# Attention's order per engine rewritten around the DVE and POOL passes of a pair

## What is computed

```python
def attn(x):                                   # x = layer norm of the input, 16 x 256 x 128
    xn = layer_norm(x, gamma_in)
    q, k, v = xn @ Wq, xn @ Wk, xn @ Wv        # 16 heads of 64
    attn = softmax(causal(q @ k.T * scale))
    out  = attn @ v
    adj  = clip(attn + eye(n), 0, 1)
    deg  = adj.sum(-1)
    feats = v
    for l in range(2):
        h = adj @ (feats @ gnn_w[l] + gnn_b[l]) / deg
        feats = gelu(h + feats)
    out = out + feats @ lin_w + lin_b
    return layer_norm(out @ Wo, gamma_out)
x = x + attn(layernorm(x))
x = x + moe(layernorm(x))                      # 8 experts, hidden 352, top 2 of softmax(router)
```

## Time and profile before

| | us |
|---|---|
| median of 3 runs | 1221.41 |
| lowest and highest | 1219.86, 1223.13 |
| the profiled execution, its own time | 1227.73 |
| its span, first to last instruction | 1226.0 |

### The profile page before, as it was taken

The page is one execution under the profiler, slowest core; times in us unless marked ns, Lnnn a source line. Parts: engine busy times, 40 slices in busy tenths (PEclk is TensorE's granted clock), DMA queues, the critical chain, the costliest instruction groups (busy, mean ns, idle before and its releaser), DMA issues.

```text
span 1226.0 us, 28122 instructions
## 1 busy us (share of the span) xinstructions
PE 1102.3 (90%) x8320; PEld 862.3 (70%) x8320; DVE 967.5 (79%) x3755; ACT 797.4 (65%) x2351; POOL 509.9 (42%) x648
## 2 busy tenths in 40 slices
PE   6999989898989999999999999999999986798994
PEld 4777767676767676766766677667676764797993
DVE  6869797979797979797979797979798884466555
ACT  6776767676667676676757675767675752464652
POOL 4425252626252525252534343434343343444444
PEclk9999999999999999999999999999999987998997
DMA  6950000000000000000000000000000012121227
GB/s 205 406 196 1 2 10 2 9 1 9 1 9 1 7 3 5 5 2 8 0 10 0 10 0 9 1 9 1 9 1 9 2 33 66 47 62 54 66 60 217
DMA packets 37311, 47.41 MB, mean 39 GB/s; under 512 B 6009, under 2 KB 28539, under 8 KB 37200
## 3 DMA queue, kind: packets, MB, share of 16 engines
q1 hardware_dynamic: 32880, 37.81, 9.7%
q0 software_dynamic: 4320, 8.47, 2.1%
HBM read 18.14 MB, written 28.58 MB: 38 GB/s over the span
## 4 chain that ended last, share of the span: by engine, by line
PE 53%; DVE 34%; issue 7%; ACT 2%; another core or an unknown queue 2%; DMA 1%; POOL 1%; DVEq 0%; SPq 0%; ACTq 0%; POOLq 0%
PE bank L628 45%; DVE ea L1400 8%; DVE eb L1403 7%; DVE nmax L1388 7%; PE bank L997 2%; DVE dT L1417 2%; DVE t L1648 2%; PE bank L764 1%; PE bank L725 1%; DVE wgt L1412 1%; DVE next_row L1770 1%; PE bank L979 1%; DVE rs L1398 1%; DVE z L1437 1%
## 5 line engine op out<-in xcount | busy, mean ns | idle before, releaser
L495 POOL TENSOR_TENSOR ea<-ea,wgt 128x256 f32<-128x256 f32 x128 | 79.7, 622 | 439.5 <-DVE wgt L1412 439.5
L1388 DVE TENSOR_REDUCE nmax<-bank 128x1 f32<-128x128 f32 (+1 forms) x512 | 151.4, 348 | 61.7 <-PE bank L628 54.7
L1113 ACT ACTIVATE ea<-bank,nmax 128x128 f32<-128x128 f32 x256 | 98.0, 383 | 83.9 <-DVE nmax L1388 55.3
L1400 DVE SCALAR_TENSOR_TENSOR ea<-ident,ssum,ea 128x128 f32<-128x128 f32 x256 | 142.7, 593 | 0.0
L628 PE MATMUL bank<-gt,vnat 128*64 128x256 f32 (+1 forms) x1024 | 113.6, 343 | 31.7 <-ACT gvT L1081 31.7
L1403 DVE SCALAR_TENSOR_TENSOR eb<-idw,ssum,eb 128x256 f32<-128x256 f32 x256 | 141.7, 588 | 0.0
L497 POOL TENSOR_TENSOR eb<-eb,wgt 128x512 f32<-128x512 f32 x128 | 135.9, 1062 | 0.0
L628 PEld LDWEIGHTS bank<-gt,vnat 128*64 128x64 f32 x1024 | 68.3, 139 | 84.4 <-issue 41.7
L1113 ACT ACTIVATE eb<-bank,nmax 128x256 f32<-128x256 f32 x256 | 125.2, 489 | 0.0
L1081 ACT ACTIVATE gt<-bank 128x512 f32<-128x512 f32 (+1 forms) x256 | 111.7, 495 | 20.1 <-remote 19.8
L628 PE MATMUL bank<-gt,g 128*64 128x256 f32 (+1 forms) x1024 | 115.2, 347 | 4.9 <-DVE z L1443 3.8
(11 more groups left out here) (231 smaller groups left out, 3164.6 us busy)
## 6 DMA issues: line engine op xcount, KB each, us to landing
slots<-zero SPq DMA_DIRECT2D x33, 520.0 KB, 14.9
zin<-slots SPq DMA_DIRECT2D x71, 65.0 KB
got<-pairs SPq DMA_DIRECT2D x8, 512.0 KB, 7.0
raw_gu<-in_guT SPq DMA_DIRECT2D x8, 352.0 KB, 3.0
out<-x_all SPq DMA_DIRECT2D x8, 256.0 KB, 2.6
pairs<-zout,zin POOLq DMA_INDIRECT x71
dn<-in_downT SPq DMA_DIRECT2D x2, 512.0 KB, 16.1
slots<-z,row_now POOLq DMA_INDIRECT x64
```

The lines of the kernel that those rows point to most:

```text
L495: nc.gpsimd.tensor_tensor(ea[:, s], ea[:, s], wgt[:, s, 0:2].unsqueeze(2).to_broadcast([P, 2, P]), ALU.mult)
L1113: done = nc.scalar.activation(e[:, s, a, :], score_bank(n, a)[:, TILE_SCORES[t]], ACT.Exp, bias=nmax[:, s, i:i + 1], accum_out=ssum[:, s, ...
L1388: done = V.tensor_reduce(nmax[:, n % 3, i:i + 1], score_bank(n, a)[:, TILE_SCORES[t]], X, ALU.max, negate=True)
L1400: V.scalar_tensor_tensor(ea[:, s, a, :], ident[:, :], ssum[:, s, a:a + 1], ea[:, s, a, :], ALU.mult, ALU.max, accum_out=den[:, s, a:a + 1])
```

## The change

The lists of calls in `batch` are written in another order on POOL, PE, ACT and DVE. No call is added or dropped, but for these: `gelu2(n)` for n of 4 and more now waits on a new semaphore `s_og`, which PE's `output_graph` raises (it frees the slot of `f2T`), and `layer1(b, 0)` waits for the last copy of `qk` (both use bank 0). `output_attended(4)` moves from the next batch's list into the batch's own.

On DVE, `weights(n)` of pair 0 stands right behind `adjacency(0)`, the adjacencies of pairs 1 and 2 stand together, and other DVE work is put between a `weights(n)` and the next `adjacency`. The output of `before` is taken up earlier (`output_bias`, `output_kept`), and so are its norms and the next batch's input norm. The core of the diff for DVE and POOL, and what differs in ACT and PE by more than order:

```diff
@@ def batch of POOL
+                graph(b, 0)
+                degrees(b, 0)
+                graph(b, 1)
+                degrees(b, 1)
+                graph(b, 2)
+                graph(b, 3)
+                degrees(b, 2)
+                degrees(b, 3)
+                graph(b, 4)
+                if after is not None:
+                    deviation(after, 0, 3)
+                if before is not None:
+                    token_power(before, 0)
+                degrees(b, 4)
...
+                graph(b, 5)
...
+                        scatter(routed, c)
+                degrees(b, 5)
+                graph(b, 6)
+                graph(b, 7)
+                degrees(b, 6)
...
+                    for e in range(0, 3):
+                        gate_up_low(e)
                 if before is not None:
                     token_power(before, 1)
...
@@ PE
                 a_d.wait(pe, b, n + 1)
-                if n >= 1:
+                if n == 0:
+                    a_qk.wait(pe, b, PAIRS)
+                else:
                     d_z1.wait(pe, b, n)
...
-                product(bank[7][:, 0:TOKENS], lwo[:, n, :], f2T[:, n % 4, :], False, False)
+                product(bank[7][:, 0:TOKENS], lwo[:, n, :], f2T[:, n % 4, :], False, False).then_inc(s_og.sem, 1)
@@ ACT
                 d_z2.wait(act, b, n + 1)
+                if n >= 4:
+                    s_og.wait(act, b, n - 3)
@@ def batch of DVE
                 maxima(b, 1, 0)
+                adjacency(b, 0)
+                weights(b, 0)
                 maxima(b, 1, 1)
-                adjacency(b, 0)
-                maxima(b, 2, 0)
-                weights(b, 0)
...
                 if before is None:
                     small_weights()
                     dve.wait_ge(w_x, 16)
                 if after is not None:
                     norm_step(after, 0)
+                maxima(b, 2, 0)
+                maxima(b, 2, 1)
+                adjacency(b, 1)
+                adjacency(b, 2)
+                weights(b, 1)
+                if after is not None:
+                    norm_step(after, 1)
+                maxima(b, 3, 0)
+                weights(b, 2)
+                maxima(b, 3, 1)
+                if before is not None:
+                    output_bias(before)
+                if routed is not None:
+                    choose(routed, 2)
+                if before is not None:
+                    output_kept(before)
+                difference(b, 0)
+                attended(b, 0)
+                adjacency(b, 3)
```

More of the change, by code:

```diff
@@ L854, in batch @@
                 scores(b, 4)
-                differences(b, 0)
-                transposes(b, 1)
+                differences(b, 1)
+                if routed is not None:
+                    places(routed, bank[7][:, PLACES], before)
+                degrees(b, 1)
+                transposes(b, 2)
                 queries_keys(b, 6)
@@ L936, in batch @@
                 if after is not None:
-                    queries_keys(after, 1)
+                    values(after, 0, b)
             def tokens_transposed(p, o, free=None):
@@ L1236, in batch @@
                 if after is not None:
-                    queries_keys(after, 1)
+                    values(after, 0)
             def tokens_transposed(p, o):
@@ new lines, in batch @@
+                if before is not None:
+                    output_kept(before)
+                difference(b, 0)
+                attended(b, 0)
+                adjacency(b, 3)
+                maxima(b, 4, 0)
+                weights(b, 3)
+                maxima(b, 4, 1)
+                difference(b, 1)
+                if routed is not None:
+                    take_places(routed, bank[7][:, PLACES])
+                attended(b, 1)
+                if routed is not None:
+                    place_tokens(routed, 0)
+                    place_tokens(routed, 1)
@@ new lines, in batch @@
+                if before is not None:
+                    norm_tokens(before, 0)
+                maxima(b, 5, 0)
+                adjacency(b, 4)
+                difference(b, 2)
+                weights(b, 4)
+                if before is None:
+                    folded_values()
+                attended(b, 2)
+                maxima(b, 5, 1)
+                if before is not None:
+                    norm_tokens(before, 1)
+                maxima(b, 6, 0)
+                maxima(b, 6, 1)
@@ new lines, in batch @@
+                adjacency(b, 5)
+                difference(b, 3)
+                weights(b, 5)
+                attended(b, 3)
+                maxima(b, 7, 0)
+                maxima(b, 7, 1)
+                layer1_out(b, 0)
+                if after is not None:
+                    norm_step(after, 2)
+                adjacency(b, 6)
+                layer1_out(b, 1)
+                difference(b, 4)
+                attended(b, 4)
+                weights(b, 6)
+                layer1_out(b, 2)
@@ L1530, in batch @@
+                adjacency(b, 7)
+                if before is not None:
+                    norm_tokens(before, 2)
+                layer2_out(b, 0)
+                if after is None:
+                    gate_up_high(0)
+                if after is not None:
+                    norm_step(after, 3)
+                layer1_out(b, 3)
+                if after is None:
+                    table_first(0)
+                weights(b, 7)
                 difference(b, 5)
                 if after is not None:
-                    norm_step(after, 1)
```

301 lines of the change are left out of this document (107 added, 194 removed).

## The result

The changed kernel takes 1183.06 us (median of 4 runs, 1182.0 to 1185.7) where the kernel before takes 1221.86 beside it: a ratio of 0.9687, with a 95% interval from 0.9666 to 0.9708. Run once more later, beside other runs of before, it had 0.9702 (0.9679 to 0.9725). The forecast was 1181.

The account below looks back on a forecast made before the run. PE's 57.73 busy us of a 62.34 us batch were taken as the floor, with DVE slowed by POOL's multiplications. 1227.73 - 36.4 + 1.5 - 5.5 = 1187.3, less 6.3 for the median: 1181; range 1150 to 1214.

Parts of the forecast that it names:

- Part 1: Front of the batch: POOL's pair 0 ends by 9.5 us, adjacency(1) and (2) take 1.5 us each, from 2.6 and 2.2.
- Part 2: DVE between pair 2's `wgt` and adjacency(3): three new waits for PE, idle 0.6, 0.2 and 0.1 us; adjacency(3) at 17.3.
- rival C: DVE's three new waits for PE decide, from about 3.5 us of delay on: slower, 1244 us; chance 0.11.
- Part 3: Middle of the batch: `transposes(4)` at 27.3 us; PE idles 0.6 at `scores(7)` and some 0.4 at `differences`.
- Part 4: POOL's four scatters, 5.0 us, hold up pair 5's `deg` and pairs 6 and 7; hidden with about a microsecond to spare.
- the marker for pair 7: Sign in the profile after: POOL's multiplications of pair 7 end ahead of 43 us of the batch.
- Part 5: Back of the batch: about 1.5 us of POOL's delay remains on the norms; graph network's round gives 0.8 us of idle.
- rival A: The contention only moves to other DVE steps; half of the 7.5 us stays on the path: 1203 us; chance 0.18.
- The sum of a batch: PE's idle time per batch falls from 4.6 to 2.0 us, 2.6 less; over 14 batches 36.4 us.
- Part 6: Batch 0: DVE waits 4.9 us for the rest of `x`, +3 (0 to +5), against a gain of 1.5: net +1.5.
- Part 7: Batch 15: `gate_up_low(2)` ahead of `token_power` saves 4 us, 1 may return, contention 1.5: -5.5 (0 to -7).
- The sum: Whole kernel: 1187.3 us for an execution like the profiled one, 6.3 lower for the median: 1181, a gain of 3.3%.

Follow-up runs that it names:

- The moved `wgt`: Changed kernel with DVE's `wgt` of pair 0 moved back behind the maxima of pair 2, right ahead of adjacency(1): 1195.1 us, ratio 0.9799 to before.
- x late: Changed kernel with DVE's wait for the rest of x in batch 0 moved behind `wgt` of pair 1: 1181.6 us, ratio 0.9654 to before.
- the old halves: Changed kernel with POOL's `gate_up_low` in batch 15 again taken in 2, 3 and 3, not 3, 3 and 2: 1186.8 us, ratio 0.9703 to before.
- the early norm: Changed kernel with DVE's norm_tokens(2) (L1656) moved ahead of adjacency(6): 1191.6 us, ratio 0.9740 to before.

## Why the prediction was right, point by point

**The mechanism** was right: DVE's passes were long because of POOL, and freeing them is 30 of 39 us. The bound was not: 4.6 us of idle time were called all that any order can take out of a batch, and without POOL's streams a batch takes 56.50 for 62.34.

**Part 1, the front.** Counted from `scores(0)` at 497.89: `wgt` of pair 0 at 7.2 (forecast 7.1), adjacency(1) and (2) from 9.7 to 12.6 (forecast 9.6 to 12.6), `scores(3)` at 11.9 (forecast 11.9). POOL and DVE there:

```profile
505.35 0.61 POOL L495 TENSOR_TENSOR ea<-ea,wgt 128x256 f32<-128x256 f32 x1 [10.35 <-DVE wgt L1420]
505.92 1.04 POOL L497 TENSOR_TENSOR eb<-eb,wgt 128x512 f32<-128x512 f32 x1
...
507.93 0.35 DVE L1408 SCALAR_TENSOR_TENSOR ea<-ident,ssum,ea 128x128 f32<-128x128 f32 x1
```

POOL's pair 0 (its `deg` too, at 507.53) has ended before DVE's passes start; in the earlier trace rows it had not. The moved `wgt` puts a price on exactly this: 12 us.

**Part 2, the three new waits.** DVE's wait in front of `yT`, and the step of `choose` behind it:

```profile
513.15 0.48 DVE L1434 TENSOR_SCALAR yT<-bank,yb 128x256 f32<-128x256 f32 x1 [0.72 <-PE bank L633]
513.55 0.91 DVE L1755 TENSOR_SCALAR ratio<-ratio 128x2 f32<-128x2 f32 x1
```

PE started the last output product at 14.6 (512.52; forecast 14.9, so rival C, which needed 3.5 us of delay, was far), DVE was idle for 0.72, 0 and 0 (forecast 0.6, 0.2, 0.1). But adjacency(3) started at 18.3, not 17.3: `choose` took 1.5 us where I had put 0.5 for its four tiny steps, since I had not asked whether a step on 2 elements is held up too. It is.

**Part 3, the middle.** PE idles for 0.52 at the differences and 0.40 at `scores(7)`, 0.9 in sum (forecast 1.0). `transposes(4)` stands at 28.2 (forecast 27.3), later by what part 2 had missed; PE has other work until then.

**Part 4, the scatters.** Pair 6 ends at 40.5 and pair 7 at 43.4 (forecast 39.9 and 41.5; the marker for pair 7, ahead of 43, was missed), PE wants pair 6 at 43.0: hidden, with 2.5 us to spare where I had seen one. In the chain, POOL does not stand in the way. That they cost nothing there is right; that they would cost 16 us at the old place was no part of the forecast.

**Part 5, the back.** The 1.5 us of contention on the norms is what came: L1656 takes 1.6 us too long. It is not hidden behind PE's full queue but stands in front of the one result that PE waits for, 1.50 us of idle where I gave 0.8. But the norms are not all that was left. DVE's busy time falls by another 70.9 us when POOL streams nothing (913.0 and 842.1), 4.4 us a batch, where the forecast left 1.5 of 7.5: `choose`, `place_tokens` and the `ve` steps (L1651 and L1358, 0.5 to 0.6 us for 0.17) now stand beside POOL. By the size of the contention that is rival A's half; most of it was not on the path, and that was not forecast. The marker "L1656 below 0.7" failed (1007 ns).

**The sum of a batch.** PE idle 2.5 us (forecast 2.0), busy 57.09 (taken as 57.73): 59.60 for 59.7. The two misses cancel. The 14 batches gave 43.4 us and not 36.4; the missing term is the clock. In before, five of the 14 batches took 63.4 to 63.9 us for 62.3, at a granted clock of 0.97, and without their excess (6.4 us) the 14 give 37.0. In one of the five, stretches of 4 us, and then the same place one batch earlier, in a batch of 62.4 us:

```profile
301.00:305.00 4.00, 2.35 (x19) 1.48 (x16) 2.32 (x10) 1.55 (x5) 3.67 (x5) 1.00 0.15 50
305.00:309.00 4.00, 3.48 (x19) 2.56 (x20) 3.76 (x7) 1.59 (x6) 2.31 (x4) 0.57 0.00 0
...
238.57:242.57 4.00, 2.44 (x19) 1.55 (x17) 2.39 (x11) 1.53 (x4) 3.62 (x5) 1.00 0.15 50
242.57:246.57 4.00, 3.46 (x32) 2.92 (x34) 3.96 (x8) 1.64 (x6) 2.38 (x4) 1.00 0.00 0
```

PE is busy for 2.35 of 4 us, and then runs the next 4 us at a granted clock of 0.57. One batch earlier it is busy for 2.44 of 4 us at the same place and stays at 1.00. So both batches have this idle time and the clock fell behind it in one only; why in some batches and not in others stays open. In the changed kernel the mean over the 14 batches is 1.00 (0.99 before). That five batches were longer was to be read from the trace of before: I had taken one batch at 1.00 for all.

**Part 6, batch 0.** The wait was forecast at 4.9 us, with the DMA landing at 28.0:

```profile
27.85 0.49 DVE L1349 BATCH_NORM_STATS2 stat<-x_all 128x6 f32<-128x128 f32 x2 [4.83 <-DMA x_all<-in_x]
29.95 0.58 PE L633 MATMUL bank<-mask,ident_bf 128*128 128x256 bf16 x2 [3.67 <-ACT eb L1118]
```

4.83, until 27.85. The wait came as forecast. The step that failed is what it costs: net +1.5 forecast, with +5 as the upper bound for the wait, and +8.0 and +6.2 measured in the two profiles. Without the wait (x late) 6.1 and 4.3 of it go, the clock's fall behind PE's 3.67 us included, and +1.9 are left where a gain of 1.5 was forecast.

**Part 7, batch 15.** The size came: -6.3 and -6.2 us measured, -5.5 forecast. The reason that was given for most of it did not. The wait for `raw_gu` was to give 4 us by the order of the halves, and with the old order put back batch 15 is only 1 to 3 us longer. What is left of the 6.3 comes from the new order of the engines' lists around it (POOL's wait for the token power is 4.43 us with the old halves, for 7.38 in the earlier trace rows); which step of it is not shown. In both orders batch 15 is 3 us shorter without POOL's streams (77.1 for 80.4, 71.0 for 74.1), so the contention is about as costly there after the change as before, and the 1.5 us counted for it did not come.

**The sum.** It started from the profiled execution of before, 1227.73, and came to 1187.3; the changed kernel's took 1183.16. The 14 batches gave 7.0 more than forecast, batch 0 cost 6.5 more (4.7 in the second profile), batch 15 gave 0.8 more, and the rest, forecast unchanged, took 3.0 less (2.3 more in the second profile). The last step took off 6.3 us, because the median of before was that far below its profiled execution. In the changed kernel the two are 0.1 apart (1183.16 and 1183.06): the step has nothing there to stand on. The five batches with the low clock make before's profiled execution long by 6.4 us, so this step and the 7 us missing in the batches may be one and the same thing; that was not shown, since one profile of before was kept. That the sum met the median within 2 us is luck in part; that a batch at full clock gives 2.7 us (62.3 to 59.6, forecast 2.6) is not.

## What to carry to other kernels

Where two engines lock each other out of a memory, a handover in program order has two costs: the work, and what the receiver's work does to the sender's next step. Let the sender hand over first and then do what needs no such access (reductions from PSUM) until the receiver has ended; a row of 0.17 us at the right place was worth 12 us here. But a list of this kind holds by timing alone: half a microsecond of shift in an unrelated step (the early norm) brought the collision back at the next place, so every move has to be looked at in both engines' timelines. And PE's idle time can have a price behind it where the clock falls: in batch 0, 3.5 us of busy time behind a wait of 3.67. Last, a sum that starts from one profiled execution should be checked against more than one batch of it.
